# Q's projection weights in four blocks, O's split moved, shared results added in other places, and one slot's weight loads ahead of the stores

## The reference

```
x = x + linear_attention(layernorm(x))          # 16 heads of 32
      q, k, v = h @ q_w.T + q_b, h @ k_w.T + k_b, h @ v_w.T + v_b
      qp, kp = elu(q) + 1, elu(k) + 1
      out = (qp @ (kp.T @ v)) / (qp . sum(kp) + 1e-6);  out @ o_w.T + o_b
x = x + long_convolution(ctx_2048, ctx_2048, layernorm(x))
x = x + moe(layernorm(x))                       # 16 experts, 4 per token
      out = sum over the 4 experts e of w_e * (silu(h @ g_e.T) * (h @ u_e.T)) @ d_e.T
      shared = silu(h @ sg.T) * (h @ su.T) @ sd.T
      result = x + out + shared
```

## Time and profile before

| | us |
|---|---|
| median of 3 runs | 926.69 |
| lowest, highest | 924.92, 928.87 |
| the profiled execution | 926.22 |
| its span, first to last instruction | 924.2 |

### The profile page before, as it was taken

One profiled execution on the slowest core, in us unless ns is written; L12 is line 12 of the kernel. 1 busy time (PEld: TensorE's weight loads), 2 busy tenths in 40 slices (PEclk: granted clock), 3 DMA queues, 4 the chain that ended last, 5 costly groups with the idle time before them and its releaser, 6 DMA issues.

```text
span 924.2 us, 14017 instructions
## 1 busy us (share of the span) xinstructions
PE 861.9 (93%) x4369; PEld 710.7 (77%) x4369; DVE 575.7 (62%) x883; ACT 375.9 (41%) x604; POOL 383.1 (41%) x385
## 2 busy tenths in 40 slices
PE   4899999999899999889999877999999999999995
PEld 3788888888777777668787765777877777778774
DVE  4557666575659999999759755454444544454431
ACT  3323222332133433333553224555555455555552
POOL 2300000001036686542523122665666566665644
PEclk9899999999999999999999999999999999999998
DMA  9400000000026534330210255898788888888757
GB/s 323 144 1 1 1 0 0 0 0 1 12 57 188 178 114 103 114 93 22 85 60 6 84 183 179 227 188 216 188 205 184 191 208 199 192 185 211 188 115 90
DMA packets 49346, 109.45 MB, mean 118 GB/s; under 512 B 8800, under 2 KB 9312, under 8 KB 49184
## 3 DMA queue, kind: packets, MB, share of 16 engines
q0 software_dynamic: 17024, 40.48, 23.2%
q1 hardware_dynamic: 32288, 68.55, 22.8%
HBM read 78.35 MB, written 30.65 MB: 118 GB/s over the span
## 4 chain that ended last, share of the span: by engine, by line
PE 64%; DVE 15%; issue 9%; ACT 5%; DMA 3%; SPq 1%; POOL 1%; POOLq 0%; DVEq 0%; ACTq 0%
PE PS L194 16%; PE PS L196 16%; PE PS L195 16%; PE PS L205 7%; DVE QY L892 4%; PE PS L1444 2%; PE PS L571 2%; ACT wh L1253 2%; PE PS L512 2%; DVE term L886 2%; DMA QY<-in_owT 1%; DVE QY_rounded L1700 1%; ACT hTh L1245 1%; DVE term L876 1%; DVE wl L1695 1%
## 5 line engine op out<-in xcount | busy, mean ns | idle before, releaser
L194 PE MATMUL PS<-QY_rounded,wh 128*128 128x512 f32 (+1 forms) x376 | 153.6, 408 | 1.9 <-DVE LG L1582 0.9
L196 PE MATMUL PS<-QY_rounded,wl 128*128 128x512 f32 (+1 forms) x376 | 146.8, 391 | 0.0
L1174 POOL DMA_INDIRECT out_y<-QY,idy x72 | 118.5, 1646 | 41.6 <-ACT QY L1264 24.5
L195 PE MATMUL PS<-QY_rounded,wh 128*128 128x512 f32 (+1 forms) x312 | 120.2, 385 | 0.0
L1710 DVE TENSOR_TENSOR hTl<-hh,hTh 128x512 fp32r<-128x512 f32 (+1 forms) x41 | 27.8, 679 | 117.3 <-ACT hTh L1245 117.3
L1156 POOL DMA_INDIRECT xg<-xs_d,idx x72 | 84.8, 1178 | 32.3 <-issue 16.1
L205 PE MATMUL PS<-qER,Tz 128*128 128x288 f32 x320 | 82.7, 414 | 8.8 <-DVE low_rounded L733 5.8
L258 POOL TENSOR_SCALAR var_eps<-mean_var 128x2 f32<-128x2 f32 x15 | 3.3, 219 | 197.9 <-DVE mean_var L369 197.9
L196 PEld LDWEIGHTS PS<-QY_rounded,wl 128*128 128x128 f32 x376 | 70.9, 189 | 15.1
L205 PEld LDWEIGHTS PS<-qER,Tz 128*128 128x128 f32 x320 | 61.1, 193 | 27.4 <-DVE low_rounded L733 6.8
L194 PEld LDWEIGHTS PS<-QY_rounded,wh 128*128 128x128 f32 x376 | 71.4, 190 | 13.9 <-ACT hh L1241 1.0
(11 more groups left out here) (207 smaller groups left out, 1852.3 us busy)
## 6 DMA issues: line engine op xcount, KB each, us to landing
ws<-in_gu_w SPq DMA_DIRECT2D x38, 512.0 KB, 5.3
ws<-in_dn_w SPq DMA_DIRECT2D x20, 512.0 KB, 5.8
C<-in_ctx SPq DMA_DIRECT2D x32, 256.0 KB, 2.6
Tz<-kpad_d SPq DMA_DIRECT2D x32, 256.0 KB, 3.3
xs_d<-xn SPq DMA_DIRECT2D x16, 256.0 KB, 2.0
out_y<-X SPq DMA_DIRECT2D x16, 256.0 KB, 5.9
X<-in_x SPq DMA_DIRECT2D x1, 3072.0 KB, 19.7
xg<-xs_d,idx POOLq DMA_INDIRECT x72, 4.5
```

The costliest lines, as they stand in the source:

```text
L194: pe.matmul(out_, lh, rh, start=first, stop=False)
L195: pe.matmul(out_, lh, rl, start=False, stop=False)
L196: return pe.matmul(out_, ll, rh, start=False, stop=last)
L1174: nc.gpsimd.indirect_dma_start(out=out, out_offset=bass.IndirectOffsetOnAxis(ap=idy[:, t:t + 1], axis=0), in_=yo[:, t], in_offset=None, co ...
```

## The change

Four things change in the order of work; nothing is computed in another way.

1. **Loads of the prologue.** x of batch 0 comes as two transfers with semaphores of their own; the first tile's statistics wait only for the first. Q's weights are laid out as four column blocks of 128 and come as four transfers with a semaphore each. Then SP waits for the second tile, the identity and Q's second block before it issues K's weights. Q's bias, V's weights and x of batch 1 go ahead of the broadcast constants; O's bias goes last, behind O's weights.
2. **Splits of the prologue.** Q is split high and low by blocks. GpSimd splits no weights any more: VectorE splits K low (behind `x_lo(0)`) and O low (in step 0, between `v_bias` and `kv_mask`); ScalarE splits O high in step 0, between `k_evac` and `x_hi`.
3. **`add_shared` on VectorE.** Group 0 goes ahead of `hidden(-1, 0)`, group 1 ahead of `hidden(-1, 1)`, group 2 ahead of the splits of slot 0's tokens, group 3 into `body(1)` behind `w_lo(1, 1)`. `hid_lo(-1, 1)` goes ahead of `w_lo(0, 1)`.
4. **SP in the third block.** The load of part 1 of slot 1 goes ahead of the stores of groups 0 to 2, that of part 1 of slot 2 ahead of the stores of group 3.

```diff
@@ sync, prologue
-            load_x(0, 1, 0)
+            sp.dma_start(X[:, 0], x[0, 0:P]).then_inc(x_first, 16)
+            sp.dma_start(X[:, 1], x[0, P:2 * P]).then_inc(x_in[0], 16)
             sp.dma_start(ident[:], c_ident).then_inc(x_in[0], 16)
-            load_w(0, qwT)
+            for c in range(DC):
+                sp.dma_start(wstage[:, 0, :, c * P:(c + 1) * P], qwT[c]).then_inc(wq_in[c], 16)
+            sp.wait_ge(x_in[0], 32)
+            sp.wait_ge(wq_in[1], 16)
             load_w(1, kwT)
-            sp.dma_start(qb[:], q_b).then_inc(consts_in, 16)
+            sp.dma_start(qb[:], q_b).then_inc(qb_in, 16)
+            load_w(2, vwT)
+            load_x(1, 2, 1)
             ... kb, vb, block, headm
-            load_w(2, vwT)
-            load_x(1, 2, 1)
             load_w(3, owT)
+            sp.dma_start(ob[:], bcast_rows(o_b)).then_inc(ob_in, 16)
@@ gpsimd, prologue
             rstd(pool, 0, 0)
-            pool.wait_ge(w_hi, 2)
-            nc.gpsimd.tensor_tensor(WL[:, 1], wstage[:, 1], WH[:, 1].bitcast(F32), ALU.subtract).then_inc(ko_lo, 1)
             rstd(pool, 0, 1)
-            pool.wait_ge(w_hi, 4)
-            nc.gpsimd.tensor_tensor(WL[:, 3], wstage[:, 3], WH[:, 3].bitcast(F32), ALU.subtract).then_inc(ko_lo, 1)
@@ scalar
                 k_evac(b)
-                if not first:
+                if first:
+                    split_hi(3)
+                else:
                     a_hi(b - 1)
...
-            split_hi(0)
+            for c in range(DC):
+                cols = slice(c * P, (c + 1) * P)
+                act.wait_ge(wq_in[c], 16)
+                act.activation(WH[:, 0, :, cols], wstage[:, 0, :, cols], ACT.Copy).then_inc(wq_hi, 1)
             x_hi(0)
-            for i in range(1, 4):
+            for i in range(1, 3):
                 split_hi(i)
@@ vector, step 0 and prologue
+                if first:
+                    dve.wait_ge(consts_in, 16 * 4)
                 k_bias(b)
...
                 v_bias(b)
-                if not first:
+                if first:
+                    w_lo_part(3)
+                    dve.wait_ge(ob_in, 16)
+                else:
                     x_add(b - 1)
...
-            w_lo_part(0)
+            for c in range(DC):
+                wq_lo_part(c)
             x_lo(0)
-            dve.wait_ge(consts_in, 16 * 6)
+            w_lo_part(1)
+            dve.wait_ge(qb_in, 16)
@@ tensor, qproj: per block c of batch 0
+                        pe.wait_ge(wq_lo, c + 1)
@@ sync, third block
                 next_part(e, 0, 0)
+                next_part(e, 0, 1)
                 for g in range(NG - 1):
                     store_group(g)
-                for part in range(1, NPART):
-                    next_part(e, 0, part)
+                next_part(e, 0, 2)
                 e = expert_of(sp, 2)
                 next_part(e, 1, 0)
+                next_part(e, 1, 1)
                 store_group(NG - 1)
-                for part in range(1, NPART):
-                    next_part(e, 1, part)
+                next_part(e, 1, 2)
@@ vector, third block
                     w_lo(s, 1)
+                    if isinstance(s, int) and s == 1:
+                        add_shared(NG - 1)
                     hidden(s, 0)
...
+                add_shared(0)
                 hidden(-1, 0)
                 hid_lo(-1, 0)
                 w_lo(0, 0)
-                add_shared(0)
+                add_shared(1)
                 hidden(-1, 1)
+                hid_lo(-1, 1)
                 w_lo(0, 1)
-                hid_lo(-1, 1)
+                add_shared(2)
                 for d in range(DC):
                     x_lo(0, d)
...
-                add_shared(1)
                 hidden(0, 0)
                 hid_lo(0, 0)
                 w_lo(0, 2)
                 w_lo(1, 0)
                 for d in range(DC):
                     x_lo(1, d)
-                add_shared(2)
-                add_shared(3)
                 body(1)
```

More of the change, by code:

```diff
@@ L135, in decoder_program @@
         x_in = [sem(f"x_in{i}") for i in range(3)]
-        w_in = [sem(f"w_in{i}") for i in range(4)]
+        x_first, qb_in, ob_in = sem("x_first"), sem("qb_in"), sem("ob_in")
+        w_in = [None] + [sem(f"w_in{i}") for i in range(1, 4)]
+        wq_in = [sem(f"wq_in{c}") for c in range(DC)]
+        wq_hi, wq_lo = sem("wq_hi"), sem("wq_lo")
         memsets = sem("memsets")
@@ L363, in ln_stats @@
                         i = b if isinstance(b, int) and b < 2 else 2
-                        wait_apart(dve, x_in[i], 32 if i == 0 else 16)
+                        if i == 0 and t == 0:
+                            wait_apart(dve, x_first, 16)
+                        else:
+                            wait_apart(dve, x_in[i], 32 if i == 0 else 16)
                     else:
@@ L471, in step, with wq_lo_part, w_lo_part @@
                     ln_norm(1, b - 1)
+            def wq_lo_part(c):
+                cols = slice(c * P, (c + 1) * P)
+                dve.wait_ge(wq_hi, c + 1)
+                dve.tensor_tensor(WL[:, 0, :, cols], wstage[:, 0, :, cols], WH[:, 0, :, cols].bitcast(F32), ALU.subtract
+                                  ).then_inc(wq_lo, 1)
+            def w_lo_part(i):
+                dve.wait_ge(w_hi, i)
+                dve.tensor_tensor(WL[:, i], wstage[:, i], WH[:, i].bitcast(F32), ALU.subtract).then_inc(w_lo, 1)
             ln_stats(0, 0)
             ln_norm(0, 0)
-            def w_lo_part(i):
-                dve.wait_ge(w_hi, i + 1)
-                dve.tensor_tensor(WL[:, i], wstage[:, i], WH[:, i].bitcast(F32), ALU.subtract).then_inc(w_lo, 1)
-            w_lo_part(0)
+            for c in range(DC):
+                wq_lo_part(c)
             x_lo(0)
-            dve.wait_ge(consts_in, 16 * 6)
+            w_lo_part(1)
+            dve.wait_ge(qb_in, 16)
             dve.tensor_scalar(nqb[:], qb[:], -1.0, None, ALU.mult).then_inc(nqb_done, 1)
@@ L523, in qproj @@
                 pe.wait_ge(xT_lo, TPB * (b + 1))
-                pe.wait_ge(kv_done, 4 * b)
+                if not (isinstance(b, int) and b == 0):
+                    pe.wait_ge(kv_done, 4 * b)
                 for c in range(DC):
+                    if isinstance(b, int) and b == 0:
+                        pe.wait_ge(wq_lo, c + 1)
                     o = PS[:, 4 + c // 2, (c % 2) * S:(c % 2 + 1) * S]
@@ L583, in step @@
                     t2(b - 2)
-                pe.wait_ge(ko_lo, 1)
+                pe.wait_ge(w_lo, 1)
                 pe.wait_ge(at_done, 2 * TPB * b)
@@ L591, in step @@
                 if not first:
-                    pe.wait_ge(ko_lo, 2)
+                    pe.wait_ge(w_lo, 3)
                     oproj(b - 1)
@@ L600, in _ @@
             t1(0)
-            pe.wait_ge(w_hi, 1)
-            pe.wait_ge(w_lo, 1)
             step(0, first=True)
@@ L1782, in lay_out @@
     vals = [
[L1783 removed]
+        f(x), f(c), f(np.asarray(L0_attn_q_w).T.reshape(DC, P, DC, P).transpose(2, 1, 0, 3)), f(np.asarray(L0_attn_k_w).T), f(np.asarray(L0_attn_v_w).T),
         f(np.asarray(L0_attn_o_w).T), f(np.asarray(L0_attn_q_b).reshape(DC, P).T), f(L0_attn_k_b), f(L0_attn_v_b), f(L0_attn_o_b),
```

3 lines of the change are left out of this document (removed).

## The result

The changed kernel takes 915.7 us (median of 4 runs, 915.0 to 917.5); the kernel before took 927.78 us beside it (4 runs, 924.92 to 929.71). The ratio is 0.9893, with a 95% interval of 0.9871 to 0.9915. The forecast was 913.4 us, in a range of 909 to 918.5. The profiled execution took 915.0 us, 913.2 of it span, so 11.2 us less than the one before; the forecast sum was 13.25.

A forecast was written before the change was run, and what follows sets the result against it. TensorE, busy for 93% of the span, bounds the kernel, so time is won only where it idles or runs at half clock. 8.05 (start) + 5.2 (third block) = 13.25 us less, giving 913.4 us, range 909 to 918.5.

The forecast's parts named there:

- rival A: Whole kernel: the result comes as forecast, 909 to 917 us; chance 0.60.
- rival C: Third block: last store as slow as today or slower, GpSimd's chain paces slot 2; 2 us less gain, 915.4; chance 0.10.
- E: Third block: it gives nothing because another PE wait takes over, such as slot 2's tokens; 918.6 us; chance 0.04.
- Part 1 and 2: Prologue: Q's projection starts at 12.3 instead of 15.75, 3.45 us; with idle time and clock 8.05 us together.
- Rival B: Start: Q's four blocks each pay a whole transfer, so Q's projection starts at 15.95; 917.0 us; chance 0.12.
- Idle time ahead of `kv` and the clock: Step 0: PE's idle time falls from 3.17 to about 0.8, 2.4 us; the clock stays up behind it, 2.2 us.
- Rival D: Step 0: the clock falls all the same after the idle time; 2.2 us less gain, 915.6; chance 0.06.
- Part 3: Third block: moved `add_shared` lets PE go straight into slot 1's down, ending at 574.0 instead of 580.14, 6.1 us.
- Part 4: Third block: moved loads are needed, or part 3's gain shrinks to 1 or 2 us; group 3's stores hardly delayed.
- What is late next: Third block: last store lands after 5.75 us instead of 8.55; waiting for slot 3's tokens takes 1.3 of 6.1 us.
- First scatter: GpSimd, third block: starts at 569 by the forecast, today 582.5; later than 573 would show the prediction wrong.
- Third block and loads together: Part 3 and 4, third block: 5.2 us won, bounds 3.3 and 6.4.

The follow-up runs named there:

- e1_start: The changed kernel's start (loads and splits of the prologue) with the third block of the kernel before; 920.38 us, ratio 0.9921.
- e5_q_whole: The changed kernel with Q's weights loaded in one transfer, still split in four blocks, K issued after all of Q; 920.03 us, ratio 0.9928.
- e6_no_sp_wait: The changed kernel with SP issuing K's weights at once, without waiting for x and two blocks of Q; 916.59 us, ratio 0.991.
- e11_o_high_early_pool: The changed kernel with O's high split ahead of step 0 on ScalarE and low splits of K and O on GpSimd; 922.78 us, ratio 0.9974.
- e7_splits_on_pool: The changed kernel with the low splits of K's and O's weights given back to GpSimd; 916.87 us, ratio 0.9908.
- e3_no_load_move: The changed kernel with both moved loads of the third block back in SP's old order; 913.3 us, ratio 0.9853.
- e8_second_move_back: The changed kernel with only the load of part 1 of slot 2's weights back behind the stores of group 3; 912.89 us, ratio 0.9854.
- e4_group3_early: The changed kernel with group 3 added and stored earlier, in pieces, and slot 2's part 1 load behind its stores; 912.03 us, ratio 0.9842.
- e2_third: The changed kernel's third block with the start of the kernel before; 922.78 us, ratio 0.9961.
- e10_o_high_early: The changed kernel with ScalarE splitting O's weights high ahead of step 0; 920.86 us, ratio 0.9947.
- e9_early_and_stores_first: `e4_group3_early` with the load of part 1 of slot 1's weights behind the stores of groups 0 to 2; 912.18 us, ratio 0.9857.

## Why the prediction was right, and where it was not

**The result lies in the range and on the forecast side**, 2.3 us above the point and inside what rival A named. The start came as forecast. The third block brought less: the condition of rival C took place (the last store about as slow as before, with 915.4 as the time), but not the wait that it names, for slot 3's tokens. What PE waited for was, in part, what E names: slot 2's tokens.

**Part 1 and 2.** Start of Q's projection: forecast 3.45 us, measured 3.47. That the two agree is in part luck, since two steps missed in opposite directions: the last block was in at 8.71, not 9.6, and the transposes ended at 10.66, not 10.2. The start hung on the transposes, not on the blocks. In ten of the eleven profiles with the new start, Q's projection begins 3.56 us behind the start of the transposes (3.77 in `e1_start`, where they are earliest), whether Q's last block is in at 8.71 or at 9.80; in the kernel before it was 6.77. VectorE works from the normalisation through the low splits to the end of batch 0 without a break, and what holds it ahead of that is the identity (the row at 5.20). So of the 3.47 us, 3.21 come from Q's weights being ready in time and 0.26 from earlier transposes. How much of the 3.21 is the cut into blocks and how much the later K is not shown; `e5_q_whole` and `e6_no_sp_wait` don't part them. Rival B is out: the four blocks landed 3.8 to 4.5 us after their issue each, flying together. The rule of the Trainium skill that stood against the cut ("DMA: Bandwidth & Descriptors", section "Bandwidth") did not decide here; one transfer of 1 MB was in 0.11 us after the last of four.

**Idle time ahead of `kv` and the clock.** Forecast 2.4 and 2.2, measured 2.34 and 2.43. The sizes are right, one reason is not. That GpSimd's split had held `qp` is true (1.3 us in `e11_o_high_early_pool`), but it is only half of what made `qp` late: it could not begin before 28.96, because ScalarE split O ahead of its copies of Q's results. Giving the splits to VectorE is not what the gain comes from: `e7_splits_on_pool` keeps them on GpSimd and shows no loss. What decides is O's high split behind those copies, which the prediction named in one sentence beside; taking that alone back costs 5.0 us. Rival D didn't take place: after 0.83 us idle the clock stayed up.

**Part 3.** Down at 574.0 instead of 580.14 was forecast, 6.1 us; measured 6.15 (14.34 less 8.19). Right, with its reason.

**Part 4.** Two steps failed. "Without part 4 the gain of part 3 shrinks to 1 or 2 us": `e3_no_load_move` is faster without it. The prediction took the load's lateness for a matter of order on SP, when it was a matter of the adds that the stores ahead of it waited for, and these part 3 moves. And of group 3's stores it said that they go out behind the load at about the time of their adds, which was to cost nothing. The issue was indeed at about that time (560.33), but the load was in flight with them and with the gathers of slot 2: undoing this move alone is worth 2.8 us in the medians.

**What is late next.** The sum took 1.3 us off for slot 3's tokens; PE had no wait there. The waits were for slot 2's tokens, 1.91 us, and for ScalarE's results behind slot 0's scatters, 0.54 us, a wait that the prediction did not have at all. The last store took 8.2 us to land, not 5.75, because "It no longer stands behind two of the loads" was wrong: one stood right ahead of it (in the kernel before there were three, issued at 568.03, 568.88 and 570.73). Without that one, in `e8_second_move_back`, the term comes out: 5.35 us. First scatter: forecast 569, measured 571.67, 2.7 us late but short of the 573 that the prediction named as a sign of being wrong. Starting it at 567.86 doesn't end the wait behind the scatters (1.71 us on PE); starting it at 562.58 does (`e4_group3_early`). Third block and loads together: forecast 5.2, measured 3.6, and 3.6 by the ratio of `e2_third` too.

**Open.** The changed kernel's runs spread over 2.5 us, those of `e3_no_load_move`, `e4_group3_early` and `e8_second_move_back` over 0.4 to 1.2. A wait at slot 0's scatters that differs from execution to execution would make such a spread: with the load ahead of the stores, PE's wait is at most 0.8 us in five profiles and 3.96 and 3.73 us in two (`e5_q_whole`, `e10_o_high_early`). That fits, but these are profiles of different kernels, one each. And `e9_early_and_stores_first`, without such a wait, spreads over 4.4.

## What to carry to other kernels

When a load is late because the queue ahead of it waits for data, look at who makes the data late before moving the load: once that is mended the load may come in time by itself, and the move can cost by putting its bytes in front of something shorter with a chain behind it. Of each transfer that is moved, ask whose landing is nearest behind it, stores and gathers too, and what its landing releases. A split or copy whose data land late belongs behind the work that waits for nothing on the same engine; here that was worth more than taking it to another engine. And where one profile is set beside another, read the distance between two rows of the same chain before the time of one row: the start of Q's projection moved by 0.8 us between kernels with the same start, and its distance to the transposes did not move.

## What the runs showed of the hardware

- After the same idle time of 2.9 us the granted clock was back at 1.00 about 3 us after the matmuls began in one kernel and about 6 us in another, with the same matmuls behind it. That made 1.07 us of difference at the first matmul of slot 0 (8.23 and 9.30 us). Idle times of 0.83, 1.71 and 1.91 us left the clock at 1.00; 3.17, 3.96 and 4.06 us were followed by 0.50.
- One 512 KB load ahead of four stores of 256 KB, issued among indirect gathers, put the first scatter 3.8 us later (571.67 against 567.86), 2.7 us of it beyond the 1.1 us by which PE itself was later.
- Equal transfers at equal issue times land differently: in profiles with the same issues ahead of it and right behind it, the identity's 64 KB took from 2.5 us (`e1_start`) to 3.6 (`e9_early_and_stores_first`), 3.4 in the changed kernel. The transposes hang on it, and Q's projection of otherwise equal starts lay between 11.73 and 12.54.
